# A decoder layer with routed experts: five weight buffers, and one of three weight splits moved to GpSimd

## The reference

```
x = x + window_attention(layernorm(x))
x = x + cross_attention(layernorm(x), context)
x = x + experts(layernorm(x))

experts(x):                       # E = 8, 256 -> 2 * 1024 -> 256
  top1 = argmax(softmax(x @ router_w + router_b))
  for i in range(E):
    h = x @ w1[i] + b1[i];  a, g = split(h)
    y = (a * sigmoid(g)) @ w2[i] + b2[i]
    out += where(top1 == i, y, 0)
```

## Time and profile before

| what | value |
|---|---|
| time, median of 3 runs | 1238.18 us (1238.03 to 1238.29) |
| the profiled execution | 1236.09 us, its span 1234.4 us |
| busy over the span: TensorE, its weight loads | 1098.6 us (89%), 915.0 us (74%) |
| VectorE, ScalarE, GpSimd | 838.1 us (68%), 587.0 us (48%), 620.3 us (50%) |
| mean granted TensorE clock | 0.968 |

### The profile page before, as it was taken

How to read it: one execution, slowest core, us unless ns; L and a number is a source line. 1 busy time by engine, 2 the same in 40 slices (tenths; PEclk the granted TensorE clock), 3 DMA queues, 4 the chain that set the end, 5 groups by cost and what they waited for, 6 DMA issues and landing times. The chain is left out here.

```text
span 1234.4 us, 21275 instructions
## 1 busy us (share of the span) xinstructions
PE 1098.6 (89%) x7718; PEld 915.0 (74%) x7718; DVE 838.1 (68%) x1517; ACT 587.0 (48%) x1000; POOL 620.3 (50%) x526
## 2 busy tenths in 40 slices
PE   4999689999998999999999999708999989899998
PEld 2655457777777778687778888607998979789887
DVE  4699347778648876568784554355888778676785
ACT  1254423545515545334455444315676656555663
POOL 6349107666538585477575122322555354453542
PEclk9999899999999999999999999958999999998999
DMA  8533301111220111201112111155576666665670
GB/s 189 147 123 124 96 20 45 47 30 47 38 62 19 37 33 36 54 12 44 33 38 46 38 39 39 22 191 173 203 242 229 213 231 214 235 229 201 230 268 29
DMA packets 94020, 134.09 MB, mean 109 GB/s; under 512 B 40929, under 2 KB 75444, under 8 KB 88029
## 3 DMA queue, kind: packets, MB, share of 16 engines
q1 hardware_dynamic: 78813, 111.68, 28.9%
q0 software_dynamic: 15104, 21.06, 6.2%
HBM read 111.50 MB, written 23.91 MB: 110 GB/s over the span
## 5 line engine op out<-in xcount | busy, mean ns | idle before, releaser
L1787 DVE TENSOR_TENSOR wlow<-staged,whigh 128x2048 fp32r<-128x2048 f32 x69 | 159.1, 2306 | 6.1 <-ACT whigh L1884 6.1
L1997 PE MATMUL psH<-xhigh,whigh 128*128 128x256 f32 x512 | 146.5, 286 | 11.4 <-DVE glow L1818 8.4
L1884 ACT ACTIVATE whigh<-staged 128x2048 fp32r<-128x2048 f32 x69 | 132.4, 1919 | 50.1 <-DMA staged<-in_L_ffn_w 50.1
L1666 POOL TENSOR_TENSOR idle<-e_less 128x1 f32<-128x1 f32 x42 | 49.8, 1186 | 195.8 <-DMA ids_now<-ids 101.5
L1997 PE MATMUL psH<-xlow,whigh 128*128 128x256 f32 x512 | 144.0, 281 | 0.0
L1997 PE MATMUL psH<-xhigh,wlow 128*128 128x256 f32 x512 | 144.0, 281 | 0.0
L1394 PEld LDWEIGHTS psD<-vo,pT 128*128 128x128 f32 x1024 | 124.8, 193 | 24.2 <-issue 20.5
L1394 PE MATMUL psD<-vo,pT 128*128 128x128 f32 x1024 | 135.0, 279 | 6.9 <-issue 5.2
L748 ACT ACTIVATE pT<-psA 77x512 f32<-77x512 f32 x128 | 75.8, 593 | 71.5 <-PE psA L1376 68.9
L1997 PEld LDWEIGHTS psH<-xhigh,whigh 128*128 128x128 f32 x512 | 98.6, 193 | 13.4 <-DVE gated L1804 9.1
L704 ACT ACTIVATE o2T<-psA 128x512 f32<-128x512 f32 x64 | 38.2, 597 | 141.8 <-PE psA L1404 141.2
(11 more groups left out here) (268 smaller groups left out, 2876.5 us busy)
## 6 DMA issues: line engine op xcount, KB each, us to landing
staged<-in_L_ffn_w SPq DMA_DIRECT2D x69, 1024.0 KB, 5.1
tokens<-out_rows POOLq DMA_DIRECT2D x32, 256.0 KB, 6.3
kT<-k_cols SPq DMA_DIRECT2D x16, 308.0 KB, 2.9
vo<-v_rows SPq DMA_DIRECT2D x16, 308.0 KB
xb<-in_x SPq DMA_DIRECT2D x32, 128.0 KB
b2s<-in_L_ffn_b SPq DMA_DIRECT2D x23, 128.0 KB
k_cols<-qT SPq DMA_DIRECT2D x4, 616.0 KB
v_rows<-pT SPq DMA_DIRECT2D x4, 616.0 KB
```

The lines of the kernel that those rows point to most:

```text
L1666: nc.gpsimd.tensor_tensor(idle[:, i:i + 1], e_less_8[:, 0:1], e_less_8[:, 0:1], ALU.add)
L1787: tt(wlow[par][:, i, :], staged[:, i, :], whigh[par][:, i, :].bitcast(F32), ALU.subtract)\
L1884: nc.scalar.activation(whigh[par][:, i, :], staged[:, i, :], ACT.Copy).then_inc(w_high[i], 1)
L1997: ins = mm(psH[:, q % 2 * PAIR + c, part, :], lhs, rhs, start=i == 0, stop=i == len(passes) - 1)
```

## The change

`staged` gets two more buffers (`staged_more`). The pieces of all tiles are numbered n = 3t + i and use buffer n mod 5; the load of piece n waits for the low part of piece n - 5. SyncE loads pieces 0 and 1 of t+3 at the start of tile t, and piece 2 of t+3 after the biases. The high parts count on one semaphore `w_high`, the low parts on `w1_split` (pieces 0 and 1, VectorE) and `w2_split` (piece 2). The low part of piece 2 is made by GpSimd (`low_second`), as its first instruction of a tile. On VectorE and ScalarE the remaining parts stand at other places in the order, depending on whether the tile is big. In TensorE's order a small tile's wait for `g_split` moves from `hidden` to `turn_gated`.

```diff
@@ -1577,6 +1578,17 @@
 
             return (t, q - 1) if q > 0 else (t - 1, PAIRS_HID - 1)
 
+        def piece(t, i):
+
+            n = t * PIECES + i
+            k = n % W_BUFFERS
+            return n, k, staged[:, k, :] if k < 3 else staged_more[:, k - 3, :]
+
+        def split_of(n):
+
+            t, i = n // PIECES, n % PIECES
+            return (w1_split, KC * t + i + 1) if i < KC else (w2_split, t + 1)
+
         def exists(t):
 
             return t < NT
@@ -1592,16 +1604,17 @@
                 slot = SLOT_OF[t]
                 return sp.value_load(tile_ei[0:1, slot:slot + 1], min_val=0, max_val=E - 1)
 
-            def load_piece(t, e, i, wait=True):
-                if wait:
-
-                    sp.wait_ge(w_split[i], t)
+            def load_piece(t, e, i):
+                n, k, rows = piece(t, i)
+                if n >= W_BUFFERS:
+
+                    sp.wait_ge(*split_of(n - W_BUFFERS))
                 if i < KC:
                     src = w1[bass.ds(e, 1), i * P:(i + 1) * P, :].rearrange("a p n -> p (a n)")
-                    sp.dma_start(staged[:, i, :], src).then_inc(w_in[i], 16)
+                    sp.dma_start(rows, src).then_inc(w_in[k], 16)
                 else:
                     src = w2[bass.ds(e, 1)].rearrange("a (k p) n -> p (a k) n", p=P)
-                    sp.dma_start(staged[:, i, :].rearrange("p (k n) -> p k n", k=HC), src).then_inc(w_in[i], 16)
+                    sp.dma_start(rows.rearrange("p (k n) -> p k n", k=HC), src).then_inc(w_in[k], 16)
 
             def load_bias(t, e):
                 par = t % 2
@@ -1636,18 +1649,20 @@
             load_bias(1, second)
             for i in range(PIECES):
                 load_piece(1, second, i)
-            load_piece(2, expert(2), 0)
+            third = expert(2)
+            for i in range(PIECES):
+                load_piece(2, third, i)
 
             def tile(t, slot, par):
-                if exists(t + 2):
-                    e = expert(t + 2)
-                    load_piece(t + 2, e, 1)
-                    load_piece(t + 2, e, KC)
+                if exists(t + 3):
+                    e = expert(t + 3)
+                    load_piece(t + 3, e, 0)
+                    load_piece(t + 3, e, 1)
                 sp.wait_ge(y_done, t + 2)
                 if exists(t + 2):
-                    load_bias(t + 2, e)
+                    load_bias(t + 2, expert(t + 2))
                 if exists(t + 3):
-                    load_piece(t + 3, expert(t + 3), 0)
+                    load_piece(t + 3, e, KC)
                 if exists(t + 4):
                     sp.wait_ge(y_stored[par], stored(t))
                     load_ids(t + 4, slot)
@@ -1705,12 +1720,22 @@
 
                             nc.gpsimd.dma_start(ys[0:1, i, half, :], b2[0:1, :]).then_inc(y_stored[i], 16)
 
+            def low_second(t):
+
+                n, _, rows = piece(t, KC)
+                pool.wait_ge(w_high, n + 1)
+                nc.gpsimd.tensor_tensor(wlow[t % 2][:, KC, :], rows, whigh[t % 2][:, KC, :].bitcast(F32), ALU.subtract)\
+                    .then_inc(w2_split, 1)
+
             def tile(t, slot, par):
+                if exists(t + 1):
+                    low_second(t + 1)
                 bias_x2(t, slot)
                 scatter(t, slot)
                 if exists(t + 4):
                     gather(t + 4, slot)
 
+            low_second(0)
             tiles(tile)
 
         @block.vector
@@ -1781,11 +1806,11 @@
             nc.vector.memset(seed[:, 0:1], 0.0).then_inc(y_done, 1)
             nc.vector.memset(seed[:, 1:2], 0.0).then_inc(h_done, 2)
 
-            def low_part(t, par, i):
-
-                dve.wait_ge(w_high[i], t + 1)
-                tt(wlow[par][:, i, :], staged[:, i, :], whigh[par][:, i, :].bitcast(F32), ALU.subtract)\
-                    .then_inc(w_split[i], 1)
+            def low_part(t, i):
+
+                n, _, rows = piece(t, i)
+                dve.wait_ge(w_high, n + 1)
+                tt(wlow[t % 2][:, i, :], rows, whigh[t % 2][:, i, :].bitcast(F32), ALU.subtract).then_inc(w1_split, 1)
 
             def low_tokens(t, par):
                 dve.wait_ge(x_high, t + 1)
@@ -1842,8 +1867,8 @@
                 for q in (2, 3):
                     gate(t, q)
                     late_low(t, q)
-                    if exists(t + 1):
-                        low_part(t + 1, 1 - par, q - 1)
+                    if IS_BIG[t] and exists(t + 1) and q == 2:
+                        low_part(t + 1, 1)
                     early_low(t, q)
                 if exists(t + 1):
                     gate(t + 1, 0)
@@ -1853,35 +1878,37 @@
                     early_low(t + 1, 0)
                     gate(t + 1, 1)
                     late_low(t + 1, 1)
+                    if exists(t + 2):
+                        low_part(t + 2, 0)
                 else:
                     late_low(t + 1, 0)
                 finish(t, slot)
-                if exists(t + 2):
-                    low_part(t + 2, par, 0)
                 if exists(t + 1):
+                    if exists(t + 2) and not IS_BIG[t + 1]:
+                        low_part(t + 2, 1)
                     early_low(t + 1, 1)
 
             locate()
-            low_part(0, 0, 0)
-            low_part(0, 0, 1)
+            low_part(0, 0)
+            low_part(0, 1)
             low_tokens(0, 0)
             dve.wait_ge(bias_in[0], 32)
             gate(0, 0)
-            low_part(0, 0, 2)
             gate_low(0, 0)
             low_tokens(1, 1)
             gate(0, 1)
-            low_part(1, 1, 0)
+            low_part(1, 0)
             gate_low(0, 1)
 
             tiles(tile)
 
         @block.scalar
         def _(act):
-            def high_part(t, par, i):
-
-                act.wait_ge(w_in[i], 16 * (t + 1))
-                nc.scalar.activation(whigh[par][:, i, :], staged[:, i, :], ACT.Copy).then_inc(w_high[i], 1)
+            def high_part(t, i):
+
+                n, k, rows = piece(t, i)
+                act.wait_ge(w_in[k], 16 * (n // W_BUFFERS + 1))
+                nc.scalar.activation(whigh[t % 2][:, i, :], rows, ACT.Copy).then_inc(w_high, 1)
 
             def high_tokens(t, par):
                 act.wait_ge(x_turned, t + 1)
@@ -1925,8 +1952,8 @@
             def tile(t, slot, par):
                 sigmoids(t, 2)
                 late_high(t, 2)
-                if exists(t + 1):
-                    high_part(t + 1, 1 - par, 2)
+                if IS_BIG[t] and exists(t + 1):
+                    high_part(t + 1, KC)
                 early_high(t, 2)
                 sigmoids(t, 3)
                 late_high(t, 3)
@@ -1936,28 +1963,33 @@
                     late_high(t + 1, 0)
                     if exists(t + 2):
                         high_tokens(t + 2, par)
-                        high_part(t + 2, par, 0)
-                    early_high(t + 1, 0)
+                    if not IS_BIG[t]:
+                        early_high(t + 1, 0)
+                        high_part(t + 1, KC)
+                    if exists(t + 2):
+                        high_part(t + 2, 0)
+                    if IS_BIG[t]:
+                        early_high(t + 1, 0)
                     sigmoids(t + 1, 1)
                     late_high(t + 1, 1)
                     if exists(t + 2):
-                        high_part(t + 2, par, 1)
+                        high_part(t + 2, 1)
                     early_high(t + 1, 1)
                 else:
                     late_high(t + 1, 0)
 
             for i in range(KC):
-                high_part(0, 0, i)
+                high_part(0, i)
             high_tokens(0, 0)
-            high_part(0, 0, KC)
+            high_part(0, KC)
             act.wait_ge(h_done, 2)
             sigmoids(0, 0)
             high_tokens(1, 1)
             gate_high(0, 0)
-            high_part(1, 1, 0)
+            high_part(1, 0)
             sigmoids(0, 1)
             gate_high(0, 1)
-            high_part(1, 1, 1)
+            high_part(1, 1)
             tiles(tile)
 
         @block.tensor
@@ -1980,14 +2012,13 @@
                 par, item = t % 2, t * PAIRS_HID + q
                 if q == 0:
                     pe.wait_ge(x_split, t + 1)
-                    pe.wait_ge(w_split[0], t + 1)
-                    pe.wait_ge(w_split[1], t + 1)
+                    pe.wait_ge(w1_split, KC * t + KC)
                     if not IS_BIG[t]:
                         pe.wait_ge(bias_in[par], biases(t))
                 pe.wait_ge(h_done, item + 1)
-                if item >= 2 and not IS_BIG[(item - 2) // PAIRS_HID]:
-                    pe.wait_ge(g_split, item - 1)
                 if IS_BIG[t]:
+                    if item >= 2 and not IS_BIG[(item - 2) // PAIRS_HID]:
+                        pe.wait_ge(g_split, item - 1)
                     for c in range(PAIR):
                         for part in range(2):
                             w = part * HID + (q * PAIR + c) * P
@@ -2011,7 +2042,10 @@
 
                 if IS_BIG[t]:
```

(16 more changed lines are left out.)

## The result

The changed kernel takes 1349.86 us (median of 4 runs, 1344.38 to 1351.58), the kernel before beside it 1238.11: a ratio of 1.0908 (95% interval 1.0862 to 1.0955). The direction and the main mechanism were as forecast, but 69 us were forecast and 112 came; the top of the range was 1332 us.

What follows compares the result with a forecast made beforehand. Two bounds almost on top of each other: TensorE and GpSimd's ring of dependences. Low part 86 - slack 26.7 - relief 21 = +38, plus queueing 32, on 1236 gives 1306, as a median 1307 us; whole range 1266 to 1332.

Steps and rivals of the forecast that it cites:

- Ring as the bound, low part inside it: GpSimd's loop from finish over tiny add, scatters, ids, gathers and b2 to next finish; low part adds 86 us.
- Relief of the tiny adds: The tiny add after VectorE's finish falls from 2.17 to 0.65 us in 14 turns, giving 21 us back.
- TensorE's removed wait: TensorE's 9.9 us of waits before hidden layers of small tiles go, but give nothing back.
- The clock's falls covered by spare time: TensorE's half speed after a gap costs 1.7 us, covered by the turn's spare time; uncovered, 32 us in all.
- Queueing of VectorE: VectorE's low part, held off by GpSimd, delays the finish after b2: 1.7 us a turn, 32 us (0 to 42).
- 26.7 us of slack: GpSimd's waits for `ys` over 19 turns, 43.0 us, less 16.3 for the finish; subtracted from the added cost.
- ScalarE's copy, taken to be in time: In small tiles ScalarE's copy of the third piece is made before GpSimd comes to it; no cost put.
- The wait for ids, taken as unchanged: GpSimd's wait for ids between scatters and gathers stays at 5.3 us a turn, 101.5 in 19.
- Scatters land later: Rival (0.06): a tile's second load flies with the next scatter; scatter to wake-up 5.6 becomes 7, another 28 us, 1334.
- forecast case: Main case (0.72): GpSimd's low part and VectorE's queueing make the kernel slower, 1307 us, own range 1284 to 1326.
- Ends taken as 0: Extra loads near the first gather, 0 taken (0 to 3 us), and tiles 20 to 22, 0 taken (0 to 8).

## Why the prediction was right in its way and wrong in its size

- **Ring as the bound, low part inside it: right, and shown.** The low part took 4.6 us (forecast 4.5) and 89.0 in all (86). Shortening it takes 87 us off, moving it in GpSimd's order (with ScalarE's third copy in small tiles) 90.
- **Relief of the tiny adds: right.** 22.4 us (21).
- **TensorE's removed wait worth nothing: right**, as `ys` takes its place (85.7 us in 20 waits).
- **The clock's falls covered by spare time: not shown, and one turn speaks against it.** The granted clock falls to 0.5 after these gaps, as in this stretch at the start of the turn shown above:

```profile
1032.70:1039.40 6.70, 5.27 (x25) 5.30 (x26) 5.47 (x7) 2.31 (x2) 4.48 (x3) 0.50 0.39 118
```

  TensorE is busy for 5.27 us of it at half speed, an estimated 2.6 us lost. Later in the same turn VectorE's low part, which comes behind the gate and so hangs on TensorE, starts 0.08 us after GpSimd's (1049.08) and is held:

```profile
1049.16 7.86 DVE L1813 TENSOR_TENSOR wlow<-staged,whigh 128x2048 fp32r<-128x2048 f32 x1
```

  With 2.6 us more in hand it would have come first. So part of the queueing below may hang on the clock; no run tells the two apart.

- **Queueing of VectorE, mis-sized.** I took 1.7 us a turn, at most 2.2, for one low part between b2 and finish. It came to 44.8 us, 2.4 a turn: b2 took 8.1 more, and b2 to the end of the finish is 51.5, of which 19 x 0.78 = 14.8 is the finish. The term left out that VectorE is in arrears by more than the low part: in 8 turns a held `glow` and a gate stand ahead of it (the finish ends 4.14 us after b2 in seven of them, as shown above), and in the 5 turns that lead to a small tile b2 itself waits some 2 us. After the 26.7 us of slack that it uses up, 32 - 26.7 = 5.3 was forecast and 18.1 came: 13 us short.
- **ScalarE's copy, taken to be in time: wrong.** In small tiles the copy of the third piece was to be made before GpSimd comes to it; GpSimd waits for it 5.1 of the row's 5.5 us, where nothing was put.
- **The wait for ids, taken as unchanged: the step that failed.** I weighed the loads by when they are needed and not by what they fly beside. The wait of 5.3 us a turn became 6.5. "Scatters land later" was a rival at 0.06, with an extra of 28 us; it came on top of the forecast case, 21.8 us. Its cause was put wrongly too: not the second load behind `low_second`, but the third piece's, whose new place is beside the scatter; moving it alone gave 37.5 us of the wait back. Without these 21.8 us the time would have been near 1328, inside the range.
- **Ends taken as 0:** 3.8 at the start (bounds 0 to 3) and 5.6 in the last tiles (0 to 8), 9.4 us.

13 + 5.5 + 22 + 9.4 + 3 (low part) - 8 (scatters, which take 68.5 us again in the run with the finish first) is the 45 us between the forecast's 70 and the 114.8. The range treated the late landing as another case than the queueing, while both are waits of the same ring and add.

## What to carry to other kernels

A chain of waits that runs through an engine with 50% busy time is worth walking once round: write down each station of the turn and its slack, and price every added instruction by its place in that order, not by its engine's load. The same subtraction on the same engine cost 90 us more before b2 than in the wait for the ids. Ask of a moved transfer also what is in flight beside it: here 1 MB started with a scatter delayed the wake-up that hangs on the scatter by 1.4 to 2.0 us a turn.

## What the runs showed of the hardware that was not expected

- A load of 1 MB started beside an indirect scatter lengthened the time from scatter to the fetched ids: on average 4.5 us (85.8 in 19) with no such load, 5.9 with piece 0, 6.5 with piece 2, all with the low part on GpSimd; 4.4 and 6.0 (piece 2) with it on VectorE in the order of the kernel before.
- When a VectorE instruction with two SBUF inputs waits for GpSimd and two GpSimd instructions follow at once, either may come first. In 13 turns with a b2 of 512 columns VectorE let both pass (8 times a `glow`, as the one of 4.50 us above, 5 times a low part). In the 5 turns with a b2 of 256 columns its low part went between them, and b2 took 2.8 us instead of 0.74:

```profile
1008.69 2.79 POOL L1699 TENSOR_TENSOR xs<-xs,b2s 128x256 f32<-128x256 f32 x1
1007.37 3.52 DVE L1813 TENSOR_TENSOR wlow<-staged_more,whigh 128x2048 fp32r<-128x2048 f32 x1
```

  What decides it was not tried.
